# A second order of the calls for the loop's iterations from the tenth on, and four products into four column groups, in a two-layer attention and feed-forward kernel

## What is computed

```python
x = x + long_convolution(ctx, ctx, layernorm(x), ssm, D)       # 16 heads of 8
x = x + ffn(layernorm(x))          # silu(gate) * value, int8 activations, ternary weights, 1024 hidden
x = x + attention(layernorm(x), ctx, mask)                     # 16 heads of 8, softmax over 256
# last step, per row of x:
xn = x * rsqrt(mean(x * x) + eps) * norm_w
logits = xn @ Wc.T / temperature                               # 512 genes
top, idx = top_k(logits, 32)
expressed = softmax(top) @ genes[idx]                          # 32 values
x = x + tanh(expressed @ Wd.T) * xn * (expressed @ Wu.T) * scale
```

## Time and profile before

| | us |
|---|---|
| median of 3 runs (608.46 to 612.29) | 609.87 |
| the profiled execution | 611.78 |
| its span | 609.8 |
| PE, DVE, ACT, POOL busy | 487.1, 453.0, 344.7, 399.9 |
| `transpose_xr` of m = 13 begins | 339.8 |
| last instruction of the last batch ends | 607.6 |

### The profile page before, as it was taken

How to read it: one execution, slowest core, us unless ns; L and a number is a source line. 1 busy time by engine, 2 the same in 40 slices (tenths; PEclk the granted TensorE clock), 3 DMA queues, 4 the chain that set the end, 5 groups by cost and what they waited for, 6 DMA issues and landing times.

```text
span 609.8 us, 11293 instructions
## 1 busy us (share of the span) xinstructions
PE 487.1 (80%) x3617; PEld 285.3 (47%) x3633; DVE 453.0 (74%) x885; ACT 344.7 (57%) x578; POOL 399.9 (66%) x711
## 2 busy tenths in 40 slices
PE   1576779988878877989889889889788788787463
PEld 1465657766655543444454444444444343333121
DVE  4564659987669977789889899898787777864341
ACT  1246724323121576778877888888665676667221
POOL 6688479999887867667788878867554551342221
PEclk9878879999789998989999999999889997978855
DMA  6950120001542257366465554563573555210100
GB/s 210 371 113 6 29 53 27 14 14 34 103 101 36 71 79 140 92 105 135 96 101 129 115 105 117 103 117 96 85 156 100 100 106 135 44 22 29 46 9 17
DMA packets 92175, 54.29 MB, mean 89 GB/s; under 512 B 14851, under 2 KB 91844, under 8 KB 92118
## 3 DMA queue, kind: packets, MB, share of 16 engines
q1 hardware_dynamic: 92118, 53.58, 40.1%
HBM read 35.64 MB, written 17.42 MB: 87 GB/s over the span
## 4 chain that ended last, share of the span: by engine, by line
PE 25%; issue 24%; POOL 23%; POOLq 14%; DVE 7%; ACT 5%; SPq 1%; DMA 0%; DVEq 0%; ACTq 0%
PE pair L275 6%; POOL kv L891 4%; PE bank L492 4%; POOLq L919 3%; DVE w_int L1543 3%; POOL w_raw L968 3%; POOLq L917 3%; POOLq L42 3%; POOL yT L848 2%; ACT cT L1228 2%; POOL w_int L45 2%; PE pair L463 2%; PE bank L384 2%; POOL toep L1032 2%; POOLq L40 2%
## 5 line engine op out<-in xcount | busy, mean ns | idle before, releaser
L1543 DVE TENSOR_REDUCE w_int<-pair 128x4 f32<-128x1024 f32 x128 | 155.2, 1213 | 44.1 <-PE pair L463 43.7
L1228 ACT ACTIVATE cT<-pair 128x1024 f32<-128x1024 f32 x128 | 130.9, 1023 | 35.0 <-PE pair L479 32.5
L275 PE MATMUL pair<-kv,toep 128*128 128x256 f32 x384 | 106.8, 425 | 20.7 <-POOL kv L891 13.8
L275 PEld LDWEIGHTS pair<-kv,toep 128*128 128x128 f32 x384 | 78.5, 214 | 38.5 <-POOL kv L891 14.8
L891 POOL TENSOR_TENSOR kv<-cT 128x512 f32<-128x512 f32 x64 | 66.0, 1038 | 19.5 <-PE pair L275 13.2
L492 PE MATMUL bank<-cT,v_aug 128*32 128x256 f32 x1024 | 74.1, 410 | 0.0
L479 PE MATMUL pair<-w_raw,KS 57*128 57x256 bf16 x512 | 51.4, 280 | 27.9 <-ACT cT L1228 18.7
L1369 DVE TENSOR_TENSOR prod<-pair,qT 128x512 f32<-128x512 f32 x64 | 43.8, 684 | 33.3 <-PE pair L275 32.9
L463 PE MATMUL pair<-KS,w_raw 54*128 54x256 bf16 x512 | 51.2, 279 | 11.2 <-DVE w_int L1543 10.7
L479 PEld LDWEIGHTS pair<-w_raw,KS 57*128 57x128 bf16 x512 | 16.8, 96 | 64.8 <-ACT cT L1228 43.3
L1177 ACT ACTIVATE w_raw<-bank,st 128x512 f32<-128x512 f32 x32 | 22.0, 687 | 40.3 <-PE bank L385 40.2
(11 more groups left out here) (168 smaller groups left out, 987.9 us busy)
## 6 DMA issues: line engine op xcount, KB each, us to landing
w_raw<-scr_q SPq DMA_DIRECT2D x32, 192.0 KB
KS<-scr_k SPq DMA_DIRECT2D x32, 192.0 KB
scr_q<-w_int SPq DMA_DIRECT2D x16, 192.0 KB, 2.4
scr_k<-w_int SPq DMA_DIRECT2D x16, 192.0 KB, 2.6
scr_o<-qT SPq DMA_DIRECT2D x64, 36.0 KB
yT<-in_x SPq DMA_DIRECT2D x4, 512.0 KB, 7.3
ctx_all<-in_ctx SPq DMA_DIRECT2D x4, 512.0 KB, 7.7
x_b<-in_x SPq DMA_DIRECT2D x16, 128.0 KB, 5.4
```

The costliest lines, as they stand in the source:

```text
L275: mm = pe.matmul(bank[:, lh * n:(lh + 1) * n], toep[:, h, (lh - sh) * P:(lh - sh + 1) * P], rhs[:, sh, :], start=(sh == 0), stop=(sh == lh))
L1228: act.activation(probs[g % 4].rearrange("p j l -> p (j l)"), SC[:], ACT.Exp).then_inc(s("scores_free"), 1)
L1543: dve.tensor_reduce(neg_max[:, :, 2 * g:2 * g + 2].rearrange("p t j -> p j t"), M[:].rearrange("p (j t s) -> p j t s", t=KL, s=L), AX.X, A ...
```

## The change

It does three things. (1) Each engine's loop is cut at m = 10; from there on a second body with the same calls in another order runs, without the convolution slots and the one-time weight calls, which have nothing left to do there. (2) The four products of `expressed` no longer accumulate: product k writes PSUM partitions 32k to 32k + 31, and `down_up` adds the four parts, since its weights `wduT` now hold the 32 rows four times. (3) For that the two weight arrays are loaded four times side by side (8 DMAs for 2), and two memsets fall away.

```diff
-        genes = sb("genes", [P, KG, P])
+        genes = sb("genes", [P, KG, GD])
-        wdu_raw = sb("wdu_raw", [P, 2, 2, GD])
+        wdu_raw = sb("wdu_raw", [P, 2, 2, KG, GD])
...
-                    pe.matmul(X7[:, 0:P], genes[:, k, :], wT[:, k, :], start=(k == 0), stop=(k == KG - 1))
+                    pe.matmul(X7[GD * k:GD * (k + 1), 0:P], genes[:, k, :], wT[:, k, :], start=True, stop=True)
...
-                sp.dma_start(wdu_raw[:, n, :, :], ...
+                for r in range(KG):
+                    sp.dma_start(wdu_raw[:, n, :, r, :], ...
...
-            pool.memset(genes[:], 0.0)
-            pool.memset(wduT[:], 0.0)
...
-            dve.wait_ge(s("small_in"), 16 * 13)
+            dve.wait_ge(s("small_in"), 16 * 19)
...
-            for m in range(B + 11):
+            for m in range(10):
...
+            for m in range(10, B + 11):
+                gate(m - 2, 0)
+                maxima(m - 7, 0)
...
```

More of the change, by code:

```diff
@@ L594, in _ @@
                 project_v(m - 6)
+            for m in range(10, B + 11):
+                gate(m - 2, 0)
+                maxima(m - 7, 0)
+                transpose_maxima(m - 8)
+                logits_product(m - 10)
+                maxima(m - 7, 1)
+                value(m - 2, 0)
+                gate(m - 2, 1)
+                transpose_y(m)
+                scores(m - 8, 0)
+                value(m - 2, 1)
+                maxima(m - 7, 2)
+                transpose_weights(m - 11)
+                scores(m - 8, 1)
+                project_qk(m - 5)
+                maxima(m - 7, 3)
+                scores(m - 8, 2)
+                values(m - 8, 0)
+                scores(m - 8, 3)
+                transpose_xq(m - 1)
+                maxima(m - 7, 4)
+                expressed(m - 11)
+                scores(m - 8, 4)
+                values(m - 8, 1)
+                maxima(m - 7, 5)
+                scores(m - 8, 5)
+                down_up(m - 11)
+                ffn_product(m - 3)
+                scores(m - 8, 6)
+                maxima(m - 7, 6)
+                values(m - 8, 2)
+                scores(m - 8, 7)
+                maxima(m - 7, 7)
+                transpose_xr(m - 9)
+                values(m - 8, 3)
+                transpose_hidden(m - 2)
+                project_v(m - 6)
         @block.sync
@@ L807, in _ @@
                 load_x(m)
+            for m in range(10, B + 14):
+                write_qk_parts(m - 7)
+                write_attention(m - 10)
+                load_max_rows(m - 9)
+                load_attention(m - 10)
+                write_inverses(m - 10)
+                write_result(m - 14)
+                load_context(m - 4)
+                load_x(m)
+                spread_inverses(m - 10)
+                load_stacked_qk(m - 7)
             for k in range(2):
@@ L1072, in _ @@
                 normalise_x3(m - 9)
+                split_maxima(m - 7)
+                normalise_x2(m - 4)
+            for m in range(10, B + 12):
+                add_output_bias(m - 2)
+                scale_parts(m - 1)
+                final_sum(m - 12)
+                chosen_weights(m - 11)
+                gate_times_value(m - 2, 0)
+                quantise_x(m - 1)
+                output_scale(m - 3)
+                gate_times_value(m - 2, 1)
+                split_qk(m - 5)
+                add_attention(m - 9)
+                normalise_x1(m)
+                down_times_xr(m - 11)
+                normalise_x3(m - 9)
+                mask_context(m - 4)
                 split_maxima(m - 7)
@@ L1617, in down_times_up @@
                     s("x7_free"), 1)
-            for m in range(B + 12):
+            for m in range(10):
                 later_sum(m - 3, 2)
```

92 lines of the change are left out of this document (82 added, 10 removed).

## The result

The changed kernel takes 615.45 us, median of 20 runs (609.82 to 622.8), beside 610.44 of the kernel before (20 runs on the same chip): ratio 1.0067, 95% interval [1.0036, 1.0098]. The forecast was 599.5, with 590 to 612. The profiled execution took 613.29 with a span of 611.5.

A forecast was written before the change was run, and what follows sets the result against it. The prediction took a ring of waits through PE, DVE and POOL, 23.6 us in m = 10 to 15, to bound the kernel, with no engine full. Its terms summed to -10.4, from 609.87 to 599.5 us, range 590 to 612.

The forecast's parts named there:

- a ring of waits: m = 10 to 15: PE 11.2 us, DVE masking 1.1 and POOL 11.3 follow one another and make the 23.6 period.
- The change in m = 11 to 15, five periods: The ring there: -1.10 on POOL, +1.0 on PE, +0.65 on DVE, so +0.55 a period, +2.8 over five.
- -1.10 on POOL: m = 11 to 15: `mask_context` leaves the ring (0.68) and the wait for `tanh_down` goes (0.42).
- +1.0 for `transpose_hidden`: m = 11 to 15: its eight transposes on PE enter the ring, adding 1.0 us a period.
- +0.65 for `first_sum`: m = 11 to 15: DVE stands 0.65 to 0.7 us for the later transposed y, delaying all up to the masked q.
- The bound that I named for this case: m = 11 to 15: if DVE makes the stall up, the period changes by -0.1 us.
- `value` 1 waits for its bank: m = 11 to 15: its copy stands behind `tanh_gate` 1, 0.74 us; upper bound of +1.3 a period.
- `o_den` comes late: Rival, 0.11: loads ahead delay it; decides from a 3.4 us landing; at 6.0, POOL waits 2.6 in m = 10 to 15; 621.
- m = 18 to 24: m = 18 to 20: `moments_x3` earlier, -1.3 each; m = 21, 22: `expressed` -1.1, -0.6, moments -0.9 each; m = 23: -0.8.
- the tail did find its next wait: Rival, 0.24: in m = 16 to 22 `maxima` or the stacked rows take over, half of 9.8 is lost; 604.4 us.
- The end: Behind the last batch's attention: the shorter `expressed` counts twice, 2 x 1.1, so -2.2 us.
- The rival that the column groups don't overlap: Rival, 0.04: `expressed` on PE keeps its cost, so the sum is -6.0 and the time 603.9 us.

The follow-up runs named there:

- the kernel with two moves alone: The kernel before with `mask_context` put behind `normalise_x3` on POOL and `quantise_hidden` behind `exps` 6 on ACT, all iterations; 600.63 us, ratio 0.9881.
- the kernel without SP's new order: The changed kernel with `copy_value` 0, strike 0 and SP's order put back, `transpose_hidden` left behind `transpose_xr`; +0.4 us a period with the clock up.
- the five of the last table: The changed kernel with `transpose_hidden`, `copy_value` 0, strike 0 and SP's order all put back (595.41 us), and four with one left: +0.4, +0.7, +0.55, +1.1 a period.
- the kernel with all four undone: The changed kernel with `transpose_hidden`, `copy_value` 0, strike 0 and SP's order put back as before; 595.41 us, ratio 0.9786.
- The filler's kernel: The changed kernel with eight matmuls that nobody reads added ahead of `transpose_xr` in the second body; 612.37 us, ratio 1.0092.

## Why the prediction was wrong

The prediction named the mechanism, a ring of waits, rightly and the direction wrongly, because of one term, the step "**The change in m = 11 to 15, five periods**", +0.55 a period; +3.65 was measured (27.25 - 23.6). Point by point:

- *The ring itself*: right. 23.6 = 11.2 + 1.1 + 11.3 before, 26.9 = 14.2 + 1.8 + 10.9 after, and the kernel with two moves alone fell by 1.0 where 1.1 was worked out.
- *-1.10 on POOL*: right, 10.2 in the kernel without SP's new order.
- *+1.0 for `transpose_hidden`*: too large. By itself 0.4, since the shortened ring falls below PE's own 22.7 without it.
- *+0.65 for `first_sum`*: it fell. The wait is there (0.39 in the changed kernel and in the five of the last table), but DVE makes it up: the masked q isn't later behind `project_qk` where the strike isn't moved, and the kernel with all four undone, which keeps this move, has 22.7. The bound that I named for this case was the right end.
- *`value` 1 waits for its bank*: named as the upper bound at 0.74 and not taken. It waits 0.72, and the move costs 0.7, so the number was right and the choice wrong. That the two agree is partly luck: of the 0.57 that the trace shows at m = 13, the last to end is `mask_denominators` behind GpSimd's later product, which the prediction doesn't have at all. The queue showed it: ACT copies the first value only behind both tanh, and PE stands at the next product into that bank.
- *Strike 0 ahead of the masking*: not in the sum at all. 0.67 us of DVE's work (L1691) was put on the ring, 0.55 measured. The prediction followed DVE up to `maxima` 1 and `first_sum`, and not the order behind it.
- *`o_den` comes late*: a rival with 0.11, and half of it came true. The load landed in 3.3 us instead of 2.5, not in 6.0, just about the 3.4 from which I had it decide: 0.60 to 1.65 of waiting in m = 12 to 15 of the changed kernel, 1.1 a period where the rest of the ring is short. A threshold that close to what three loads more would do deserved a term in the sum, not a chance.
- *The clock*: not in the sum either. I took every duration at the upper level because m = 10 to 15 had 1.00 in the earlier trace rows. With the ring's closing wait moved onto PE (I even forecast about 1.5 us of it), part of the following work ran at the lower level, which put 1.6 us of longer instructions into the ring itself; that made the ring longer again, and the wait 2.07. The filler's kernel shows its size: 2.15 a period.
- *m = 16 and 17*: forecast -2.4, measured (25.1 + 23.6) - 46.2 = +2.5, for the same reasons.
- *m = 18 to 24*: the forecast's terms from m = 18 to 23 sum to -8.2, and -9.2 was measured up to 23, -10.3 with 24. That agreement is luck. By iteration, m = 18 to 20 gave -3.2, -2.8 and -0.6 where -1.3 each was forecast, m = 21 gave -2.6 for -2.0, and m = 22 and 23 gave 0.0 for -1.5 and -0.8. Part of what m = 18 and 19 gave is the clock: the kernel before has granted clocks of 0.86 and 0.92 in them, the changed kernel 1.00 in both, and nothing in the forecast speaks of that. In m = 22 and 23 the tail did find its next wait: GpSimd's `add_attention` waits 6.01 and 7.42 for the load of `o_den` before, and 7.10 and 6.41 after, a wait that the forecast's chain through `expressed` leaves out.
- *The end*: forecast -2.2, measured -5.0. PE in the last batch but one, first of the kernel before, then after:

```profile
579.99 0.69 PE L513 MATMUL bank<-ident,qT 128*128 128x128 f32 x2 [7.57 <-POOL qT L920]
581.15 3.78 PE L521 MATMUL bank<-wcT,qT 128*128 128x512 f32 x4 [0.47 <-ACT qT L1242]
...
589.92 2.07 PE L545 MATMUL bank<-wduT,exprT 128*128 128x512 f32 x2 [0.37 <-ACT exprT L1278]
```

```profile
587.53 3.17 PE L522 MATMUL bank<-wcT,qT 128*128 128x512 f32 x4 [0.47 <-ACT qT L1307]
...
591.49 0.63 PE L531 MATMUL bank<-ident,toep 128*128 128x128 f32 x4 [0.78 <-ACT toep L1315]
...
592.80 0.42 PE L539 MATMUL bank<-toep,genes 128*32 128x128 f32 x8 [0.69 <-ACT toep L1337]
...
593.63 1.12 PE L546 MATMUL bank<-wduT,exprT 128*128 128x512 f32 x2 [0.40 <-ACT exprT L1343]
...
603.20 0.65 PE L539 MATMUL bank<-toep,genes 128*32 128x128 f32 x8 [0.69 <-ACT toep L1337]
```

  The clock came up within the logits, so the transposes (0.63 against 1.09), `expressed` (0.42 against the 2.07 of the earlier trace rows) and `down_up` (1.12 against 2.07) ran at the upper level: 0.6 + 0.5 + 1.65 + 0.95 = 3.7, and the last batch's `expressed` gives 2.07 - 0.65 = 1.4 more. The mechanism was right, the size of the clock's part missing. That the clock came up there is partly luck too: the end is 22.5 to 24.8 in the 14 kernels here that have the groups and the new order in their last batches, 23.8 in eight of them, and 22.6 is near the short end.
- *`expressed`*: 0.42 and 0.65, less than the 0.5 to 0.55 and 0.95 taken. The rival that the column groups don't overlap is out. In the trace's single records of L539 at 592.80 the first four products start within 0.02 us of each other and run for 0.30 each, side by side; the weight loads of the other four start 0.03 to 0.05 behind the first product, while those four run, and all share their rows. So 0.42 / 8 = 53 ns is a mean and not what one pair takes. The rule of the Trainium skill, "TensorE: Matmul & The Clock Gate", Part 3 (The mechanism), that a load overlaps a running matmul only where the row group differs, doesn't hold for this row.

Two slips in the working change nothing: DVE is taken as free at 345.71 + 1.13, where the row has 1.23, and the iteration of 20.9 us is called 19. What the range missed is the sum: +18.2 in m = 11 to 17 for +0.4, against -5 more gained behind.

## What to carry to other kernels

Where a loop is held by a ring, follow every engine's whole stretch of it, in both orders, up to the instruction that hands on; each move behind or ahead of that instruction is a term, and a wait that "the nearest row" prices belongs in the sum unless a row shows who makes it up. Then ask on which engine the ring's remaining wait will lie: if on PE, price the work behind it at the lower clock as the upper bound. A new order can be better and worse in two stages of one loop; cut it at the stage's border before judging it.

## What the runs showed of the hardware that I had not expected

- PE's granted clock fell behind idle stretches of 1 to 2.3 us between busy ones, and not always: it fell behind 0.96 in one kernel and stayed up behind 1.93 in another. In the changed kernel it fell behind all five waits of 1.71 to 2.34. It can fall a call later than the one looked at: `values` 1.07, then `transpose_hidden` 1.97. With 1.67 us of useless products in the gap it never fell in m = 12 to 15, and the periods became shorter.
- Undoing one of several moves that share a ring doesn't give its cost. `copy_value` 0 gave 0.1 undone in the changed kernel and costs 0.7 alone; SP's order gave 2.2 and costs 1.1. Leaving one in a repaired kernel gave costs that add up to within 0.4 us.
- The eight matmul instructions of `expressed` take 0.42 us in four column groups at the upper clock, where eight of full width took 1.16. Four of them, one per group, run side by side.
- `mask_denominators`, a TENSOR_TENSOR of DVE on 128x32 values in SBUF, ends 0.03 to 0.06 us behind the end of GpSimd's 128x512 TENSOR_TENSOR whenever that one runs as it starts, and takes 0.17 to 0.18 us when it doesn't. That holds in all 18 kernels of this study, from 260 to 500 us. In the changed kernel it took 0.97 to 0.99 in m = 10 to 15, in the kernel before 0.45 to 0.51. Reductions of DVE on PSUM (L1639, 1.20) ran beside the same GpSimd operation at their usual length. So a move that shifts a GpSimd operation can lengthen a small DVE operation on the ring with no semaphore between them, and the profile shows it as busy time, not as a wait.
- Open: why the groups alone, with no instruction moved, brought the lower clock to m = 12 and 13, and what decides in the last batches when the clock comes up (the end is 22.5 to 24.8 in the 14 kernels that have the groups and the new order there).
